# Dealing out graph 2's sort over graph 1's groups with a weight of 400 instead of 320 for a placed column

## What is computed

```python
x = x + gnn(layernorm(x), edges=(src, dst))             # graph 1: 100000 edges, dst sorted
x = x + ffn(layernorm(x)[None], edges=L0_ffn_edge_index) # graph 2: 131072 random edges, ids below 8192

# gnn: 8 heads x 32 channels
h = (x @ W).reshape(N, 8, 32)
alpha = leaky_relu(a_src[src] + a_dst[dst], 0.2)
attn = softmax of alpha over the edges of one dst
out = segment_sum(h[src] * attn, dst) + bias + x ; elu ; layernorm

# ffn: the same attention with 4 heads x 4 channels gives 4 expert scores per node,
# the best two are kept and softmaxed, and four experts gelu(x @ W1 + b1) @ W2 + b2 are summed by them
```

## Time and profile before

| | |
|---|---|
| time, median of 3 runs (lowest to highest) | 2412.19 us (2410.57 to 2414.98) |
| time of the profiled execution, and its span | 2410.95 us, 2409.2 us |
| PE busy over the span | 1989.9 us (83%) |
| DVE busy | 1851.8 us (77%) |
| POOL busy | 1604.6 us (67%) |
| ACT busy | 826.4 us (34%) |
| mean granted clock of PE | 0.930 |

### The profile page before, as it was taken

One profiled execution on the slowest core, in us unless ns is written; L12 is line 12 of the kernel. 1 busy time (PEld: TensorE's weight loads), 2 busy tenths in 40 slices (PEclk: granted clock), 3 DMA queues, 4 the chain that ended last, 5 costly groups with the idle time before them and its releaser, 6 DMA issues.

```text
span 2409.2 us, 36897 instructions
## 1 busy us (share of the span) xinstructions
PE 1989.9 (83%) x9787; PEld 1255.0 (52%) x9787; DVE 1851.8 (77%) x5336; ACT 826.4 (34%) x2023; POOL 1604.6 (67%) x1778
## 2 busy tenths in 40 slices
PE   5766787768989889888876787999998999899926
PEld 3534444445555555555543565665655555555515
DVE  7588999889999999999977974665555555555567
ACT  3431111113333323333313653444433444343313
POOL 0476777777777777666774636777777777777710
PEclk9988999789999989999988878999999999999968
DMA  6354444444444444444463002233222332222259
GB/s 196 105 142 112 127 125 128 128 130 128 124 125 122 125 121 117 119 120 117 116 167 113 5 7 58 71 79 86 66 70 71 94 70 66 68 70 67 65 192 355
DMA packets 159142, 263.13 MB, mean 109 GB/s; under 512 B 41783, under 2 KB 81525, under 8 KB 158933
## 3 DMA queue, kind: packets, MB, share of 16 engines
q0 software_dynamic: 61376, 124.22, 22.3%
q1 hardware_dynamic: 97556, 136.47, 17.7%
HBM read 219.59 MB, written 40.98 MB: 108 GB/s over the span
## 4 chain that ended last, share of the span: by engine, by line
PE 28%; DVE 14%; issue 11%; POOL 7%; DMA 2%; DVEq 1%; ACT 0%; ACTq 0%; SPq 0%
PE pb L1289 10%; PE pb L1303 9%; DVE x_sb L2509 4%; PE pb L1391 2%; POOL tab L724 2%; PE pb L1276 2%; POOL dl L724 2%; POOL early L724 2%; DVE big L1684 1%; PE pb L1407 1%; DVE x_sb L1942 1%; DMA big<-Y 1%; DVE Gb L1720 1%; DVEq L2644 1%; DVE adt L1690 1%
## 5 line engine op out<-in xcount | busy, mean ns | idle before, releaser
L790 POOL DMA_INDIRECT Gb<-table,idx x560 | 570.5, 1019 | 233.0 <-issue 153.0
L1303 PE MATMUL pb<-Gb,early 128*128 128x256 f32 x1568 | 396.9, 397 | 48.9 <-DVE idx L2578 48.9
L1289 PE MATMUL pb<-big,Gb 128*128 128x512 f32 (+1 forms) x832 | 413.5, 612 | 10.4 <-DVE acc L1843 9.7
L1391 PE MATMUL pb<-Gb,Sall 128*128 128x264 f32 x1120 | 354.9, 419 | 38.8 <-DVE big L1684 37.5
L1303 PEld LDWEIGHTS pb<-Gb,early 128*128 128x128 f32 x1568 | 289.5, 194 | 137.0 <-DVE idx L2578 62.6
L2509 DVE TENSOR_SCALAR x_sb<-iota,x_sb 128x394 bf16<-128x394 f16 x1024 | 360.1, 397 | 0.0
L790 POOL DMA_INDIRECT early<-table,idx x272 | 278.1, 1022 | 100.3 <-issue 74.3
L1276 PE MATMUL pb<-x_sb 128*128 128x394 bf16 x1024 | 298.2, 334 | 43.2 <-DVE x_sb L2509 40.0
L724 POOL DMA_INDIRECT dl<-table,idx x224 | 220.5, 984 | 87.4 <-issue 64.6
L867 ACT ACTIVATE early<-pb,b1c 128x512 f32<-128x512 f32 (+1 forms) x208 | 137.6, 662 | 399.5 <-PE pb L1289 399.2
L857 ACT ACTIVATE x_sb<-pb 128x512 f16<-128x512 f32 x256 | 152.9, 597 | 350.7 <-PE pb L1268 350.7
(11 more groups left out here) (468 smaller groups left out, 3136.1 us busy)
## 6 DMA issues: line engine op xcount, KB each, us to landing
Sall<-dlT SPq DMA_DIRECT2D x186, 256.0 KB, 3.4
Y<-idx SPq DMA_DIRECT2D x96, 256.0 KB, 2.2
big<-Y SPq DMA_DIRECT2D x16, 1024.0 KB, 11.2
x_sb<-in_x_dram SPq DMA_DIRECT2D x8, 1536.0 KB, 16.7
Gb<-table,idx POOLq DMA_INDIRECT x560
early<-table,idx POOLq DMA_INDIRECT x480
out_dram<-x_sb SPq DMA_DIRECT2D x24, 256.0 KB
Gb<-in_L_ffn_W_dram SPq DMA_DIRECT2D x8, 512.0 KB, 6.3
```

The lines of the kernel that those rows point to most:

```text
L790: g.indirect_dma_start(out=G1[i % 3][:, k, :], out_offset=None, in_=g1.table, in_offset=bass.IndirectOffsetOnAxis(ap=g1.idx[:, c:c + 1], a ...
L1289: t = pe.matmul(pbank[b][:, 0:nt * 128], W1s[:, w, k, f * 128:f * 128 + 128], xT[:, t0:t0 + nt, k * 128:k * 128 + 128], start=k == 0, stop ...
L1303: t = pe.matmul(pbank[b][:, 0:D], hh[:, bi % 2, f, j * 128:j * 128 + 128], W2s[:, w, f, :], start=f == 0, stop=f == 3)
L1391: t = pe.matmul(sbank[m % 3][:, 0:g1.R], S1[:, i % 2, k, :], G1[(i - 2) % 3][:, k, :], start=first, stop=last)
```

## The change

The weight of each step of the placing loop goes from 320 to 400. Nothing else is changed: every engine runs the same instructions on the same data, and only the slots in which the sort's steps stand move.

```diff
@@ -400,7 +400,7 @@
                     ops += [("turn", j // 16)] if j % 16 == 0 else [("hot", j // 4)] if j % 4 == 2 else []
                 if 6 <= j < 2 * HB + 6:
                     ops.append(("onehots", j - 6))
-                yield 320, ops
+                yield 400, ops
                 if j == HB + 7:
                     for n in range(4):
                         yield 3000, [("decode", 0, n)]
```

## The result

The changed kernel takes 2396.14 us (median of 6 runs, 2394.64 to 2397.97) against 2414.95 us for the kernel before (6 runs, 2410.57 to 2416.55): a ratio of 0.9925, with a 95% interval of 0.9912 to 0.9938. It is faster by 0.75%. The prediction was 2412.7 us in a range of 2404 to 2421, with most of the chance on no change: wrong, by 16.6 us. The profiled execution took 2394.8 us (span 2393.0, clock 0.928; before 2410.95, 2409.2 and 0.930).

A forecast was written before the change was run, and what follows sets the result against it. DVE was taken as the bound in nearly all 99 groups; +2.8 (gap), +2.8 (slower columns), -5.1 (gather waits) and 0 summed to +0.5 us, so 2411.45 us profiled, 2412.7 us as median, range 2404 to 2421.

The forecast's parts named there:

- the slower columns: Placing groups: single columns lengthened while a gather is issued; 0 to +5.6 us, middle taken, +2.8 us.
- The gap after scoring: DVE idle between line 1712 and line 1684, a 1.18 us floor from the register load; sum +2.8 us.
- The waits for gathers: DVE's waits before and at the first columns go because POOL gets ahead; -5.1 us, bounds -5.1 and 0.
- mask groups: Groups with masks and copies, now denser: 11.1 us a group, over POOL's 10.73.
- Counting masks: Groups 0 to 3, thirteen masks instead of twelve, DVE waiting for PE's counting matmuls; 0 taken, -2.9 to +2.9 us.
- The end: From the last decode on, the loop ends a fixed time after group 98, everything behind shifting as a whole; 0.
- Work moved: All DVE sort work stays inside the same 99 groups, so fewer columns a group gain nothing by themselves; 0.
- Placing groups of 11.05 us: Sign that the forecast is right: about 11.05 us a placing group with two columns in slot 2.
- group 99 within 4 us of where it was: Sign that the forecast is right: line 1698 of group 99 starts within 4 us of its earlier time.
- the wrong case: Gather waits near 490 us, placing groups under 10.6 or over 11.3 us, or over 2 us change behind 1290 us.
- The fast one: Placing groups: slow ones are no matter of slot 2, new groups run like the fast kind; 2402 us, chance 0.17.
- The slow one: Group 32, before the first column: POOL gains no lead, gather waits stay; +5.6 us, 2418 us, chance 0.25.

The follow-up runs named there:

- the pattern at weight 400: Changed kernel with column-only groups dealt by a fixed pattern, three columns in slot 2; 2389.05 us, ratio 0.9899 against the kernel before (2414.04 us).

## Why the prediction was wrong

**The step that failed is the slower columns.** The prediction took +2.8 us, with bounds of 0 and +5.6. Measured it is -12.6 us, from 22.3 to 9.7. The two ends came from two pictures, hits that go with the gathers or hits that go with the kind of group, and in both the changed kernel could not have fewer hits. The text said that the new groups of 16 and 17 columns are like neither kind, and still gave no bound below nothing; the largest gain that the rows allowed, all long columns gone, was never worked out, and it was 22.3 us. The nearest evidence was in the same trace: the 0.2 us a group that two dealings of the same 18 columns differed by already pointed to a number of hits that hangs on the dealing. With -12.6 in place of +2.8 the sum is -14.9 us, and the forecast 2396 for the profiled execution, against 2394.8.

**The Trainium skill's rule on the shared port** (page SBUF — State Buffer, section "SBUF: two separate sides") stood behind the value 0: the loser waits for the whole other instruction, so that hits go with gathers and with the time in columns. The runs bear out that gathers are what holds the columns up (395 ns with them, 379 without), and contradict the rest: the hold is at most 0.24 us (606 less 364 ns) of a gather of 0.95 us, none of the 188 columns that started in the first 0.4 us of a gather was held, and the number of hits fell from 182 to 66 with as many gathers.

**Right in kind, too small.** The gap after scoring was forecast at +2.8 us. Slot 2 of the changed kernel waits or stands empty in 26 groups and not in 27, so the working should have given +1.8. DVE's waits ahead of line 1684 over groups 0 to 98 grew by 5.2 us, from 50.0 to 55.2. The distance is as forecast: 1.18 to 1.19 us in the median with no column, with two and with three, in both kernels. But in the kernel before, long columns in slot 2 had filled part of the gap: behind two columns 0.31 us of it were idle in the median, against 0.37 in the changed kernel. Its cause, the register load, is shown by moving it.

**Right.** The waits for gathers: 5.1 us ahead of 1194 us forecast to go, and gone; mask groups 11.17 us for 11.1 forecast, groups 22 to 32 10.70 for 10.64. Counting masks: 3.7 us in 9 waits instead of 2.9 in 5, within the bounds; with line 2337, whose wait fell from 2.3 to 0.4 us, it is 1.1 less. The end: group 99 to the last instruction within 2.7 us. Work moved, 0: no run measures this term by itself; the sum below leaves little room for it.

**Forecast signs that came out the other way.** Placing groups of 11.05 us (measured 10.83), and group 99 within 4 us of where it was (13.5 us earlier). The sign named for the wrong case, placing groups under 10.6 us, wasn't reached either: the truth lay between 10.6 and 11.05, where the text had no case. The sum of the measured terms, +5.2, -12.6, -5.1 and -1.1, is -13.6 us, and groups 0 to 98 are 12.3 us shorter; 1.3 us are not accounted for.

**The rivals.** The fast one (2402 us) had the sign, and for the wrong reason: it held that slot 2 doesn't matter, while the gap stood there as reckoned. The slow one is out: no wait for a gather stayed from 402 to 1194 us.

What stays open: what a gather does at the moments at which it holds a column, and so whether a dealing could be worked out that meets none. Whether POOL loses what DVE wins isn't settled either: the 337 gathers of groups 46 to 87 took 341.9 us before and 349.5 after, 7.6 us more where the long columns took 7.6 us less, but 342.1 with the pattern at weight 400 and 343.7 at weight 434, which have few long columns too.

## What to carry to other kernels

Where two engines disturb one another, the number of hits isn't a property of the work: it hangs on which instruction stands where, so bound it by all hits gone and all instructions hit, and count hits one by one rather than by the mean or the maximum of a line. Place a sequencer's load ahead of work that doesn't need it, not between two instructions of the bound engine; that one move won more than any dealing (33 us of 2416, against 26 for weight 434). And look at the second engine before adding up gains, with its pace taken from the stretch in question: at 10.6 to 10.8 us a group the gathers took over, and improvements that had each paid alone no longer added.

## What the runs showed of the hardware

- Whether a column is long depends on when it starts within a gather. In groups 46 to 87 of the kernel before, 97 of 231 columns that started 0.4 to 0.9 us after a gather's start were above 0.42 us, 18 of 72 at 1.1 to 1.3 us, and none of the other 415; in the changed kernel 35 of 167, 29 of 95 and none of 400. This is worked out from the starts in both traces.
- The hold ends at a fixed moment. In the kernel before, 79 of the 166 columns that started 0.40 to 0.65 us after a gather's start were held. The later they started, the shorter they were (from 0.606 down to 0.432 us), and they all ended 1.03 to 1.08 us after the gather's start; in the changed kernel 28 of 118, with the same ends.
- Where a column that started there was not held, the gather was often the longer one: none of the gathers under the 79 held columns took over 1.0 us, but 45 of those under the 87 others did; 76 of 90 in the changed kernel, 78 of 80 at weight 434, where only 3 columns were held. It looks as if one of the two gives way; no run separates this, and the gathers' times are rough.
- The load of registers costs DVE next to nothing when its 0.95 us are passed under queued work: line 1684 idled 11.0 us in 42 groups with it behind the last scoring instruction, 0.3 us with it ahead of the score.
- The same kernel took 2414 to 2416 us in some sets of runs and 2739 us in another, and in that one no change to DVE's dealing could be told from none. From 900 to 1180 us of the kernel with weight 434 the granted clock was 0.91 there and 1.00 in the faster set.
